# Toeplitz tiles of a 51x51 depthwise convolution: 24 instead of 32, and the channels' matmuls in turns over four column groups

## The reference, cut to what matters

```python
B, C, H, W = 32, 32, 16, 16
# weight_comp: (C, 13 * 13), kpe: (1, 1, 51, 51), IDX_MAP: 51*51 -> 13*13
weight = weight_comp[:, IDX_MAP].reshape(C, 1, 51, 51) + kpe
x = x + depthwise_conv(group_norm(x), weight, pad=25)     # one filter per channel
```

## Time and profile before

| | |
|---|---|
| median of 3 runs | 716.51 us (715.46 to 717.93) |
| the profiled execution | 714.17 us, of which the span of its instructions is 712.3 us |
| TensorE busy | 587.6 us, 82% of the span |
| VectorE, ScalarE, GpSimd busy | 424.8, 299.7 and 119.2 us |
| the convolution stage | from 101.7 us to 169.97 us of the span |
| mean granted TensorE clock | 0.916 of full speed |

### The profile page before, as it was taken

The page is one execution under the profiler, slowest core; times in us unless marked ns, Lnnn a source line. Parts: engine busy times, 40 slices in busy tenths (PEclk is TensorE's granted clock), DMA queues, the critical chain, the costliest instruction groups (busy, mean ns, idle before and its releaser), DMA issues. The chain is left out here.

```text
span 712.3 us, 15241 instructions
## 1 busy us (share of the span) xinstructions
PE 587.6 (82%) x6314; PEld 359.2 (50%) x6314; DVE 424.8 (60%) x704; ACT 299.7 (42%) x458; POOL 119.2 (17%) x217
## 2 busy tenths in 40 slices
PE   0767889997999779878888879898998899899971
PEld 0556644673999654235555544425543654355310
DVE  3668865703322438867788837655766586667641
ACT  0355644011322120025888844244555455455540
POOL 0124420000000000031556600001220122023100
PEclk9875999999987978998899997899999999999976
DMA  7300041012000019000000000000000000000001
GB/s 217 33 2 2 4 183 13 1 46 74 1 1 1 0 39 200 1 1 1 1 2 3 2 1 1 20 12 2 1 2 10 2 1 2 9 1 2 2 6 63
DMA packets 23987, 17.17 MB, mean 24 GB/s; under 512 B 17353, under 2 KB 22505, under 8 KB 23274
## 3 DMA queue, kind: packets, MB, share of 16 engines
q1 hardware_dynamic: 23194, 13.54, 8.0%
q10 hardware_dynamic: 720, 2.56, 0.9%
HBM read 9.76 MB, written 2.13 MB: 17 GB/s over the span
## 5 line engine op out<-in xcount | busy, mean ns | idle before, releaser
L1828 DVE TENSOR_REDUCE R<-ps 128x4 f32<-128x1024 f32 x48 | 57.6, 1211 | 35.1 <-PE ps L1470 35.1
L1679 ACT ACTIVATE R<-ps 128x1024 f32<-128x1024 f32 x48 | 49.2, 1024 | 63.7 <-PE ps L1481 63.7
L1296 POOL TENSOR_TENSOR R<-R 128x512 f32<-128x512 f32 x32 | 45.4, 1419 | 48.3 <-DVE R L1232 48.3
L1837 DVE RECIPROCAL R<-R 128x256 f32<-128x256 f32 x24 | 41.9, 1746 | 14.9 <-ACT R L1672 14.9
L1481 PE MATMUL ps<-tmpA,R 32*128 32x256 f32 x384 | 50.6, 380 | 0.0
L1232 DVE TENSOR_TENSOR R<-ps,lasting 128x512 f32<-128x512 f32 x64 | 41.2, 686 | 12.9 <-PE ps L1164 12.9
L1470 PE MATMUL ps<-R,tmpA 32*128 32x256 f32 x384 | 48.9, 407 | 0.0
L1265 ACT ACTIVATE R<-R 128x1536 f32<-128x1536 f32 x32 | 47.3, 1477 | 0.1
L1603 PE MATMUL ps<-R,early 32*128 32x512 f32 x160 | 38.6, 704 | 7.8 <-PEq L1636 4.6
L1164 PE MATMUL ps<-R,Q 32*128 32x128 f32 (+1 forms) x512 | 31.2, 358 | 14.4 <-ACT R L1281 14.4
L85 PE MATMUL ps<-lasting 128*128 128x512 f32 x80 | 39.6, 655 | 3.3 <-PEq L1310 2.1
(11 more groups left out here) (290 smaller groups left out, 1203.1 us busy)
## 6 DMA issues: line engine op xcount, KB each, us to landing
R<-z SPq DMA_DIRECT2D x16, 256.0 KB, 5.0
R<-in_qv SPq DMA_DIRECT2D x1, 2560.0 KB
x<-in_x SPq DMA_DIRECT2D x4, 256.0 KB, 6.9
scratch_x<-R SPq DMA_DIRECT2D x8, 128.0 KB, 2.2
Q<-scratch_x SPq DMA_DIRECT2D x1, 1024.0 KB, 5.4
out<-x SPq DMA_DIRECT2D x4, 256.0 KB, 2.5
lasting<-in_lasting ACTq DMA_DIRECT2D x1, 811.0 KB
early<-in_early ACTq DMA_DIRECT2D x1, 793.5 KB
```

The costliest lines, as they stand in the source:

```text
L1296: pool.tensor_tensor(diagonal(u), diagonal(u), diagonal(u), ALU.mult).then_inc(diag_squared[1], 1)
L1679: act.activation(m.et[:, g % 2, 2 * i:2 * i + 2, :], ps[:, 4:6, :], ACT.Exp).then_inc(sg["exp_done"], 1)
L1828: dve.tensor_reduce(m.mx[:, g, 2 * a:2 * a + 4], ps[:, a:a + 2, :].rearrange("p i (s m) -> p (i s) m", s=S), AXX, ALU.max).then_inc(sg["ma ...
L1837: dve.reciprocal(m.yz[:, g, N:2 * N], m.yz[:, g, N:2 * N]).then_inc(sg["inv_done"], 1)
```

## The change

**Tiles.** Half 1's rows 8 to 15 hold the same numbers as half 0's rows 0 to 7, since only the offset counts. `T` now has 24 tiles along one axis: tiles 0 to 7 are half 1's rows 0 to 7, tiles 8 to 23 half 0's rows 0 to 15, and half 1 reads tiles 0 to 15. The eight tiles that both halves read (8 to 15) hold the own part alone and are copied by ScalarE. The 16 others get the position part added while VectorE carries them from PSUM, so the copy becomes an addition with an operand repeated over the channels.

**Channels.** A channel has two own matmuls of 256 columns and, for the shared tiles only, two position matmuls of 128 columns. They are issued in four steps, and in each step the four channels of a bank take their turn, each in its own column group.

**The way out.** The first half of the channels is stored and reloaded, in four DMAs of 16 partitions each, while the second half is computed. The second half's four stores and four reloads are shared between SyncE's queue and ScalarE's.

```diff
-    NT = H * S
+    HR = H // S
+    NT = H + HR
+    order = [(t, by_act) for i in range(HR) for t, by_act in ((i, False), (HR + i, True), (H + i, False))]
+    made_by = [[n for n, (_, by_act) in enumerate(order) if by_act == who] for who in (True, False)]
+
+    def source(t):
+
+        return (1, t) if t < HR else (0, t - HR)
+
+    def store(eng, h, cc):
+
+        dst = m.scratch_x.rearrange("b (ci cc) n -> cc b ci n", cc=4)[cc]
+        eng.dma_start(dst[:, 4 * h:4 * h + 4, :], m.co[32 * cc:32 * cc + 32, 4 * h:4 * h + 4, :])\
+            .then_inc(out_stored[h], 16)
+
+    def reload(eng, h, j):
+
+        eng.dma_start(m.tmpB[32 * j + 16 * h:32 * j + 16 * h + 16, :].rearrange("p (g n) -> p g n", g=G),
+                      m.scratch_x.rearrange("(g j) c n -> j c g n", j=J)[j][16 * h:16 * h + 16])\
+            .then_inc(out_loaded, 16)
...
-            for h in range(2):
-                sp.wait_ge(out_copied, 4 * (h + 1))
-                for cc in range(4):
...
-            sp.wait_ge(out_stored, 8 * 16)
-            sp.dma_start(m.tmpB[:, :].rearrange("p (g n) -> p g n", g=G),
-                         m.scratch_x.rearrange("(g j) c n -> (j c) g n", j=J)).then_inc(out_loaded, 16)
+            sp.wait_ge(out_copied, 4)
+            for cc in range(4):
+                store(sp, 0, cc)
+            sp.wait_ge(out_stored[0], 4 * 16)
+            for j in range(J):
+                reload(sp, 0, j)
+            sp.wait_ge(out_copied, 8)
+            for cc in range(2):
+                store(sp, 1, cc)
+            sp.wait_ge(out_stored[1], 4 * 16)
+            for j in range(2):
+                reload(sp, 1, j)
...
-                for cc in range(4):
-                    c = 4 * ci + cc
-                    o = ps[32 * cc:32 * cc + 32, (4 + ci) % 8, 0:N]
-                    for s in range(S):
-                        lhsT = zt[:, s * G * 128 + c:(s + 1) * G * 128:C]
-                        rhs = T[:, s, :, :].rearrange("p y (c x) -> p y c x", c=C)[:, :, c, :]
-                        pe.matmul(o, lhsT, rhs, start=(s == 0), stop=False)
-                        mm = pe.matmul(o, lhsT, m.kmat[:, s, :], start=False, stop=(s == S - 1))
+                for step, half in (("own", 0), ("shared", 0), ("shared", 1), ("own", 1)):
+                    for cc in range(4):
+                        c = 4 * ci + cc
+                        o = ps[32 * cc:32 * cc + 32, (4 + ci) % 8, 0:N]
+                        lhsT = zt[:, half * G * 128 + c:(half + 1) * G * 128:C]
+                        if step == "own":
+                            first = HR * (1 - half)
+                            rhs = T[:, first:first + H, :].rearrange("p y (c x) -> p y c x", c=C)[:, :, c, :]
+                            mm = pe.matmul(o, lhsT, rhs, start=(half == 0), stop=(half == 1))
+                        else:
+                            cols = slice(half * HR * W, (half + 1) * HR * W)
+                            pe.matmul(o[:, cols], lhsT, m.kmat[:, half, cols], start=False, stop=False)
                 mm.then_inc(out_ready, 1)
...
+            act.wait_ge(out_copied, 8)
+            for cc in range(2, 4):
+                store(act, 1, cc)
+            act.wait_ge(out_stored[1], 4 * 16)
+            for j in range(2, J):
+                reload(act, 1, j)
...
-                dve.tensor_copy(T[:, s, y, :], ps[:, w % 4, :]).then_inc(t_copied_v, 1)
+                dve.tensor_tensor(T[:, t, :].rearrange("p (c x) -> p c x", c=C),
+                                  ps[:, w % 4, :].rearrange("p (c x) -> p c x", c=C),
+                                  m.kmat[:, half, None, y * W:(y + 1) * W].broadcast_to([128, C, W]),
+                                  ALU.add).then_inc(t_copied_v, 1)
...
-            dve.wait_ge(out_loaded, 16)
+            dve.wait_ge(out_loaded, 8 * 16)
```

More of the change, by code:

```diff
@@ L655, in peripheral_convolution, with wait_tile @@
     out_copied = sem("cv_out_copied")
-    out_stored = sem("cv_out_stored")
+    out_stored = [sem(f"cv_out_stored_{h}") for h in range(2)]
     out_loaded = sem("cv_out_loaded")
     added = sem("cv_added")
-    NT = H * S
+    HR = H // S
[4 more added lines that the diff above has]
+        return (1, t) if t < HR else (0, t - HR)
+    def wait_tile(eng, n):
+        who = 0 if order[n][1] else 1
+        eng.wait_ge((t_copied_a, t_copied_v)[who], made_by[who].index(n) + 1)
+    def store(eng, h, cc):
[6 more added lines that the diff above has]
+            .then_inc(out_loaded, 16)
     with nc.Block() as block:
@@ L691, in _ @@
                       start=True, stop=True).then_inc(turned, 1)
-            for w in range(NT):
-                y, s = divmod(w, S)
+            for w, (t, _) in enumerate(order):
+                half, y = source(t)
                 if w < 4:
@@ L696, in _ @@
                 else:
-                    pe.wait_ge(t_copied_a if w % 2 == 0 else t_copied_v, (w - 4) // 2 + 1)
+                    wait_tile(pe, w - 4)
                 for i in range(3):
-                    mm = pe.matmul(ps[:, w % 4, :], m.onehot[s][:, (R - y) * W:(R - y + 8) * W], m.bparts[s][:, i, :],
+                    mm = pe.matmul(ps[:, w % 4, :], m.onehot[half][:, (R - y) * W:(R - y + 8) * W], m.bparts[half][:, i, :],
                                    start=(i == 0), stop=(i == 2))
                 mm.then_inc(t_ready, 1)
-            pe.wait_ge(t_copied_a, NT // 2)
-            pe.wait_ge(t_copied_v, NT // 2)
+            for n in range(NT - 4, NT):
+                wait_tile(pe, n)
             pe.wait_ge(rel_loaded, 16 * S)
@@ L728, in _ @@
                                ACT.Copy).then_inc(yt_copied, 1)
-            for w in range(0, NT, 2):
-                y, s = divmod(w, S)
+            for w in made_by[0]:
                 act.wait_ge(t_ready, w + 1)
-                act.activation(T[:, s, y, :], ps[:, w % 4, :], ACT.Copy).then_inc(t_copied_a, 1)
+                act.activation(T[:, order[w][0], :], ps[:, w % 4, :], ACT.Copy).then_inc(t_copied_a, 1)
             for ci in range(C // 4):
@@ L741, in _ @@
             dve.tensor_copy(m.kmat[:, :, :].rearrange("p s n -> p (s n)"), ps[:, 4, :]).then_inc(turned_copied, 1)
-            for w in range(1, NT, 2):
-                y, s = divmod(w, S)
+            dve.wait_ge(turned_copied, 1)
+            for w in made_by[1]:
+                t = order[w][0]
+                half, y = source(t)
                 dve.wait_ge(t_ready, w + 1)
-                dve.tensor_copy(T[:, s, y, :], ps[:, w % 4, :]).then_inc(t_copied_v, 1)
+                dve.tensor_tensor(T[:, t, :].rearrange("p (c x) -> p c x", c=C),
+                                  ps[:, w % 4, :].rearrange("p (c x) -> p c x", c=C),
+                                  m.kmat[:, half, None, y * W:(y + 1) * W].broadcast_to([128, C, W]),
+                                  ALU.add).then_inc(t_copied_v, 1)
             dve.wait_ge(turned, 2)
@@ L1953, in place @@
     m.w2sum = view(B * 33, "", [B, 33], base=Q_)
-    m.big = view(0, "", [S, H, CH])
+    m.big = view(0, "", [H + H // S, CH])
     m.co = view(3 * r + 4608, "", [C // 4, N])
```

3 lines of the change are left out of this document (removed).

## The result

The changed kernel takes 697.1 us, the median of 4 runs (695.99 to 698.79), against 715.99 us for the kernel before beside it (714.43 to 717.93). The ratio is 0.9724 [0.9693, 0.9755]: 19.8 us faster, between 17.5 and 22.0. The prediction was 689.7 us in a range from 685.5 to 696.0. The direction was right, the gain was put 7 us too high, and the time lies 1.1 us above the range. The profiled execution took 695.99 us with a span of 694.2.

A forecast was written before the change was run, and what follows sets the result against it. TensorE, busy for 82% of the span, was taken to bound the kernel. Savings of 5.2 (tiles), 20.0 (channels) and 1.6 us (way out) sum to 26.8, so 716.51 becomes 689.7 us, range 685.5 to 696.0.

The forecast's parts named there:

- Tiles: Tile part of the stage: eight of 32 tiles go at 0.648 us each, 5.18 us saved if TensorE stays slowest.
- Channels: Channel matmuls: shorter records and four column groups at a time bring 20.0 us, with output copies 1.3 us apart.
- The way out: From the end of the last output copy to the next stage: 11.9 us shrinks to 10.3, 1.6 us saved.
- The rival of slow additions: VectorE's additions in the tiles take 1.2 us instead of 0.69, tiles gain only 0.6 us, total 694.3; chance 0.03.
- The choice between two and four at a time: Channels' overlap: four at a time, 10.3 us, taken (chance 0.80); rival two at a time, 20.7 us, total 700.1 (0.07).
- a sign that it is wrong: Way out: a time from reload to VectorE's first add of over 5.5 us would show the prediction wrong.
- between nothing and 0.9 us more, I take 0.4: Way out: extra time for the second half's stores with the first half's reloads in flight, taken as 0.4 us.
- Half the bytes cost 1.8 us at that rate ... I take 2.5, so 4.4 in all: Second half's reload: 2.5 us of transfer plus 1.9 fixed, 4.4 us to the first add, bounds 3.7 and 5.5.
- The third term: Second half's stores, two on each queue: 0.88 us of issue plus 1.78, 2.66 us until the reloads could issue.
- The cover that failed: Before the next stage: TensorE's idle time behind the filling matmuls shrinks from 2.64 us to about 1.
- more than 3 us of change in the stages that are not edited: Unedited stages: a change of more than 3 us there would also make the prediction fail.
- Its own bounds: Around 689.7 us: cap by filling matmuls 0.8 us less gain, late DMA tail 1.6 more, clock 3 either way.

The follow-up runs named there:

- noturns: The changed kernel with each channel's four steps issued one behind the other again, without turns; 707.23 us, ratio 0.9890.
- nofirst: The changed kernel without the first half's four reloads, so half the output is not reloaded; 555.56 us, which says nothing as a whole.
- actstores: The changed kernel with all four of the second half's stores on ScalarE's queue; 696.46 us in one run.
- oldtail: The changed kernel with the old way out, all stores on SyncE and one reload; 692.6 us, ratio 0.9687.
- wide4: The changed kernel's way out with only four reloads, over all 128 partitions after the stores; half the output not reloaded; 692.34 us.
- narrow8: The changed kernel with its eight reloads of 16 partitions all issued after all stores, four on each queue; 699.36 us in one run.
- after2: The changed kernel once more, unedited, for a second profile and more timed runs; 696.57 us, ratio 0.9736.
- onlyturns: The kernel before with nothing changed but the channels' matmuls issued in turns; 700.83 us, ratio 0.9777.
- before2: The kernel before once more, unedited, for a second profile; 717.38 us.
- wide8: The changed kernel with eight reloads after all stores, each over all 128 partitions, as narrow8 but for their shape; 691.08 us in one run.
- fill15: The changed kernel with 15 filling matmuls instead of 11; 697.35 us, ratio 0.9717.
- fill15_2: The changed kernel with 15 filling matmuls again, on the same chip as after2; 693.93 us, ratio 0.9686.

## Why the prediction was right in direction and short in size

**Tiles: right.** 5.0 us saved against 5.2 forecast, at 0.644 us a tile against 0.648. The addition with the repeated operand takes 0.69 us, the price that the prediction took from the earlier trace rows, and VectorE still waits for TensorE. The rival of slow additions is out.

**Channels: right.** 19.9 us against 20.0; copies 1.30 us apart as forecast. The choice between two and four at a time was the largest in the sum, and the earlier trace rows decided it rightly. Both directions confirm it: turns put into the old kernel (1.73 us for four channels, 16.0 us gained), and turns taken out of the new one (2.83 us).

The Trainium skill ("TensorE: Matmul & The Clock Gate", Part 3) states that matmuls start and end strictly in program order, and gives 3.07 times for four tiles of 32 rows. Four channels of 5.16 us in a row would take 1.68 us at that rate, an estimate, and they take 1.30, 4.0 at a time. The order is contradicted by the loops without turns: with it a channel of 1.29 us in a row could share only its last record of 0.215 us with the next channel and would take some 1.1 us, an estimate, and noturns needs 0.71.

**The way out: the step that failed.** The prediction gave 7.5 us from the last output copy to the first add, 3.1 to the issue of the reloads and 4.4 from there. Measured were 5.5 and 5.7, together 11.2, more than the 9.04 of before. The prediction had named a reload to first add of over 5.5 us as a sign that it is wrong, and the sign came. Two terms of it were mis-sized, and a third by less.

The first is "between nothing and 0.9 us more, I take 0.4" for second stores that run beside the first half's reloads. Without those reloads the stores landed after 3.27 us, with them after 5.52 (nofirst): 2.25 us. Late issue explains at most about 0.3 of it (actstores).

The second is "Half the bytes cost 1.8 us at that rate ... I take 2.5, so 4.4 in all". A reload of half the bytes in narrow pieces took 5.7 us, no less than the 5.5 of a whole megabyte in one DMA (oldtail). The same bytes in as many wide pieces took 3.45 (wide4), so the shape costs some 2.2 us, and 2.3 with eight pieces (8.24 against 5.98). About 0.7 of that lies behind the last packet and not in the rate. The nearest row, 210 GB/s between strips of 32 partitions, was too fast for 16 partitions: narrow8 shows 151 to 162.

The Trainium skill ("SBUF — State Buffer", "Door 1: The DMA port swizzle") states that DMA bandwidth depends on how many of 16 ports the partitions reach. The direction agrees with these runs. The prediction's estimate from it, 8 of 16 ports and so half of 435 GB/s, does not: the changed kernel's second reloads moved 153 GB/s from 140.50 to 143.80. Nor can the ports of all pieces together be what counts, since narrow8's eight pieces reach all 128 partitions between them and moved 162 GB/s. Whether the ports of each single piece are, no run shows.

The third term is the stores with nothing in their way, 2.66 us from the last output copy to the next issue. Nofirst and noturns show 3.27 and 3.28, 0.6 us more. It took 1.78 us from the last issue on, as in the earlier trace rows; with two queues it is 2.4.

Together the first two cost some 4.5 us against the 6.8 that wide4 shows for as many bytes in wide reloads after the stores, and the forecast had 1.1 us of that in it (0.4, and 2.5 less 1.8).

**The cover that failed.** "The 2.64 us of idle TensorE shrink to about 1." They grew to 4.8 us with the tail, and the next stage's first four matmuls started at the half level: 2.1 to 2.4 us more. This comes with the idle time that the late adds leave: fifteen filling matmuls take it away while the DMAs stay as they are, and the median beside after2 is 2.6 us lower. But the old tail wouldn't have been safe either: oldtail and onlyturns idle for 2.77 and 2.82 us, hardly more than the 2.64 of before, and both pay 1.7 us at L116.

**The sum.** 26.8 forecast, less 3.7 for the tail, 0.3 for tiles and channels, 2.4 for the clock: 20.4, against 19.8 measured by ratio. The two profiles differ by less, 18.1 us: the stage begins 0.7 later, and behind L116 another 1.6 are lost. Both are within what two profiles of one kernel differ by (before and before2, 2.8 us behind the stage). The prediction had also named more than 3 us of change in the stages that are not edited as a sign against it; it was 4.0, of which 2.4 is L116.

**The range.** It took its upper bound from the tail of before (5.5 us from reload to add), as if a changed tail could not be slower than the old one. For the clock it held 3 us of chance, and nothing for a fall that the tail itself brings. Its own bounds also add up to 685.9 and 694.3 (0.8 less, 1.6 more, and 3 either way), not to the 685.5 and 696.0 that it states.

**What stays open.** Why a packet of 1,024 bytes takes twice as long into narrow pieces as into wide ones, with the DMA engines busy in both. And whether first-half reloads in wide shape, under the channels, would gain or lose: the channels of the first half are only 16 of the 32 partitions in each strip, so no piece of them covers all partitions, and this wasn't tried.

## What to carry to other kernels

Where small matmuls write separate column groups, issue them in turns, one for each group: that alone was worth 16 us here (12.4 to 19.5), with no work removed. A transfer that is moved under compute isn't free when the transfers that end the stage use the same DMA engines, as 2.25 us of delay showed here. A transfer that is split into pieces of 16 partitions can take as long for half the bytes as the whole did: here it paid to keep every piece over all partitions and, by the profile, to split by what the consumer reads first. When an edit makes a tail longer, look at the clock of the first matmuls behind it too.

## What the runs showed of the hardware

- Records of four column groups in turns run four at a time: 1.30 us for 5.16 us of work, 1.73 for 6.88.
- Packets of 1,024 bytes took 46 ns each in reloads over all 128 partitions (wide8, wide4, oldtail) and 89 to 118 in reloads of 16 partitions (medians, eight profiles).
- One of the first half's four reload issues took 1.62 us in the changed kernel, where the others took 0.30 to 0.44; it was 1.36 to 1.77 in after2, fill15, fill15_2 and actstores, and 0.43 in noturns, with the DMA engines about as busy (share 0.27 from 138.17 to 139.90, against 0.26 in the changed kernel from 132.28 to 135.20). The cause stays open.
- After idle TensorE, L116 ran at the full level in the profiles with 0.39, 0.57, 1.11, 1.77, 2.37, 2.54 and 2.64 us of idle time, and at the half level, in part or whole, with 2.57, 2.61, 2.77, 2.82, 2.94, 4.82, 4.84, 4.96 and 5.17 us. The two lists overlap, so the idle time just ahead is not all that counts.
